# Attention and FP4 feed-forward on one core: row maxima six pair slots ahead of the exps instead of eight

## What is computed

```python
def reference(x, Wqa, Wqb, Wkva, Wkvb, Wout, bout, w_gate, w_up, w_down):
    xn = layernorm(x)
    # attention: 16 heads of 8 features, 4 key/value heads, causal, rotary positions
    q = rope((xn @ Wqa @ Wqb).reshape(b, s, 16, 8))
    kv = (xn @ Wkva @ Wkvb).reshape(b, s, 4, 8, 2)
    k, v = rope(kv[..., 0]), kv[..., 1]          # each repeated for 4 heads
    w = softmax(causal(q k^T * 8 ** -0.5))
    att = (w v) @ Wout + bout
    # feed-forward: inputs and weights of each linear layer are rounded to FP4 in blocks of 16
    h = silu(fp4_linear(xn, w_gate)) * fp4_linear(xn, w_up)
    return x + att + fp4_linear(h, w_down)
```

## Time and profile before

| | us |
|---|---|
| median of 3 runs | 814.58 |
| lowest and highest run | 814.21, 816.49 |
| span of the profiled execution | 812.0 |
| TensorE busy | 731.3 |
| VectorE busy | 637.4 |
| POOL busy | 613.8 |
| ScalarE busy | 545.0 |

### The profile page before, as it was taken

One profiled execution on the slowest core, in us unless ns is written; L12 is line 12 of the kernel. 1 busy time (PEld: TensorE's weight loads), 2 busy tenths in 40 slices (PEclk: granted clock), 3 DMA queues, 4 the chain that ended last, 5 costly groups with the idle time before them and its releaser, 6 DMA issues.

```text
span 812.0 us, 18601 instructions
## 1 busy us (share of the span) xinstructions
PE 731.3 (90%) x6541; PEld 445.5 (55%) x6541; DVE 637.4 (78%) x1378; ACT 545.0 (67%) x1154; POOL 613.8 (76%) x707
## 2 busy tenths in 40 slices
PE   2366989999999999999999999999999999999782
PEld 1233545666656565656656565656566565656242
DVE  5569888989888888889898888888898888788200
ACT  1212777768777777777787777677777777575850
POOL 5533697878788897978787887979787888748470
PEclk9978899999999999999999999999999999999996
DMA  4423233333343334343333433343333433330211
GB/s 112 121 57 102 56 100 97 94 101 100 98 116 93 92 113 101 118 105 90 96 108 99 117 95 84 114 104 113 90 94 102 113 90 100 93 93 29 57 48 41
DMA packets 84438, 76.06 MB, mean 94 GB/s; under 512 B 27282, under 2 KB 66162, under 8 KB 84346
## 3 DMA queue, kind: packets, MB, share of 16 engines
q1 hardware_dynamic: 84346, 74.87, 33.9%
HBM read 40.73 MB, written 27.53 MB: 84 GB/s over the span
## 4 chain that ended last, share of the span: by engine, by line
PE 65%; DVE 8%; ACT 7%; DMA 6%; POOL 5%; issue 4%; SPq 4%; POOLq 0%; ACTq 0%; DVEq 0%
PE pv_ps L1109 16%; PE exp_ps L1088 12%; PE max_ps L1073 9%; PE misc_ps L1125 7%; PE max_ps L1074 5%; PE misc_ps L1166 5%; DVE neg_max L713 4%; PE misc_ps L1133 3%; ACT P L909 3%; DMA o_sum<-o_scr 2%; PE misc_ps L1164 2%; PE misc_ps L1152 2%; SPq L418 2%; PE misc_ps L1142 2%; DMA o_scr<-oT 1%
## 5 line engine op out<-in xcount | busy, mean ns | idle before, releaser
L713 DVE TENSOR_REDUCE neg_max<-max_ps 128x1 f32<-128x512 f32 (+3 forms) x768 | 430.6, 591 | 82.8 <-PE max_ps L1074 80.4
L909 ACT ACTIVATE P<-exp_ps 128x512 f32<-128x512 f32 x512 | 295.0, 599 | 166.4 <-PE exp_ps L1088 166.1
L1088 PE MATMUL exp_ps<-Q,K 128*128 128x512 bf16 (+3 forms) x1024 | 243.6, 301 | 9.0 <-ACT P L909 6.7
L1073 PE MATMUL max_ps<-K,Q 128*128 128x384 bf16 (+2 forms) x768 | 199.4, 278 | 24.6 <-DVE neg_max L713 13.5
L1074 PE MATMUL max_ps<-Kd,Q 128*128 128x128 bf16 x1024 | 190.9, 221 | 1.8 <-DVE neg_max L713 1.6
L529 POOL TENSOR_SCALAR_AFFINE_SELECT P<-P 128x512 f32<-128x512 f32 x256 | 162.8, 673 | 27.1 <-ACT P L912 27.1
L1109 PE MATMUL pv_ps<-P,V 128*32 128x512 f32 (+3 forms) x2048 | 164.2, 438 | 1.0 <-POOL P L529 0.8
L1073 PEld LDWEIGHTS max_ps<-K,Q 128*128 128x128 bf16 x768 | 75.1, 100 | 103.0 <-DVE neg_max L713 53.1
L1074 PEld LDWEIGHTS max_ps<-Kd,Q 128*128 128x128 bf16 x1024 | 97.9, 99 | 45.7 <-issue 23.0
L561 POOL TENSOR_TENSOR h<-gate_sb,up_half 128x352 f32<-128x352 f32 x64 | 59.8, 935 | 64.4 <-DVE gate_sb L726 64.4
L1088 PEld LDWEIGHTS exp_ps<-Q,K 128*128 128x128 bf16 x1024 | 81.8, 98 | 42.1 <-ACT P L909 20.5
(11 more groups left out here) (108 smaller groups left out, 989.7 us busy)
## 6 DMA issues: line engine op xcount, KB each, us to landing
Q<-q_scr SPq DMA_DIRECT2D x64, 224.0 KB
o_scr<-oT SPq DMA_DIRECT2D x32, 256.0 KB, 3.5
q_scr<-q_split SPq DMA_DIRECT2D x16, 384.0 KB, 2.6
Kd<-K SPq DMA_DIRECT2D x64, 96.0 KB
x_in<-x SPq DMA_DIRECT2D x16, 256.0 KB, 4.6
q_scr<-q_split SPq DMA_DIRECT2D x16, 256.0 KB, 2.9
x_res<-x SPq DMA_DIRECT2D x16, 256.0 KB, 5.7
o_raw<-o_scr SPq DMA_DIRECT2D x32, 128.0 KB
```

The source lines that it names most:

```text
L713: nc.vector.tensor_reduce(neg_max[:, pr // 4, i, heads[0]:heads[0] + len(heads), pr % 4], max_ps[r % 3][:, 0:len(heads) * n].rearrange("p ...
L909: nc.scalar.activation(P[g % 2][:, hh + r % 2, col:col + 512], ps[:, :], ACT.Exp, scale=SCALE).then_inc(exp_done, 1)
L1073: nc.tensor.matmul(ps[:, col:col + d], Qt, Kt[:, half, g, 0:d], start=True, stop=True)
L1088: last = nc.tensor.matmul(exp_ps[n % 2][:, col:col + width], K[par][:, half, pr // 2, kb * 128:(kb + 1) * 128], Q[par][:, pr, kb * 128:S], ...
```

## The change

The maxima move two slots back. In slot s TensorE and VectorE work on pair s - 2 of batch T+1 for s of 2 or more, and in slots 0 and 1 on pairs 6 and 7 of batch T (max_place). What hangs on the maxima moves with them:

- split_high on ScalarE: the half of pairs 4 to 7 from slot 0 (after exp tile 0) to slot 2 (after exp tile 1), the other from slot 4 (after tile 2) to slot 6 (after tile 1).
- split_rest on POOL: each goes between the first and second two causal selects of a group (group 0 and group 2).
- mrow1 goes from point 0 to point 2 of slot 2, mrow0 from point 1 to point 2 of slot 6.
- SP: place_max comes after gather_sums instead of ahead of it, and copy_k comes behind place_max, for the half whose maxima are done, instead of behind load_q.

The waits of reduce_tile, max_tile and copy_k use the new offsets.

```diff
--- before.py
+++ after.py
@@ -56,17 +56,23 @@
 MISC = [
     [[("gate0", 0, 1), ("up0", 1, 1)], [("xnT", 1, 2)], []],
     [[("q", 1, 2)], [("gate1", 0, 1), ("up1", 1, 1)], []],
-    [[("mrow1", 0, 0), ("qrot", 1, 2)], [("kk", 0, 2)], []],
+    [[("qrot", 1, 2)], [("kk", 0, 2)], [("mrow1", 0, 0)]],
     [[("gate2", 0, 1), ("up2", 1, 1)], [("v", 1, 2)], []],
     [[("gate3", 0, 1), ("up3", 1, 1)], [], []],
     [[("xqT", 1, 2)], [("out0", 0, -1)], []],
-    [[("out1", 0, -1)], [("mrow0", 1, 1)], []],
+    [[("out1", 0, -1)], [], [("mrow0", 1, 1)]],
     [[("hqT0", 1, 0)], [("hqT1", 0, 0)], [("hqT2", 1, 0)]],
 ]
 
 H_POWERS = [(2, 2), (2, 3), (2, 4), (3, 2)]
 PV_BLOCKS = ((0, 3), (1, 2))
 FIRST_T, LAST_T = -3, B
+LAG = 2
+
+
+def max_place(slot):
+
+    return int(slot >= LAG), (slot - LAG) % NPAIR
 
 
 class Step:
@@ -394,11 +400,11 @@
                                   ap=[[E * S, NSLOT + 1], [NPAIR * S, D], [1, NPAIR // 2 * S]])
                     sp.dma_start(Q[i][r:r + (NSLOT + 1) * D, 4 * hf:4 * hf + 4, :], src).then_inc(qk_loaded[hf], 16)
 
-            def copy_k(T, hf):
-
-
-                T.wait(sp, k_loaded[hf], 16 * LOAD_K, 2, 16 * LOAD_K)
-                T.wait(sp, max_filled, NPAIR * NMAX, 1, (hf + 1) * NPAIR // 2 * NMAX)
+            def copy_k(T, off, hf):
+
+                i = T.par(off)
+                T.wait(sp, k_loaded[hf], 16 * LOAD_K, off, 16 * LOAD_K)
+                T.wait(sp, max_filled, NPAIR * NMAX, off - 1, (hf + 1) * NPAIR // 2 * NMAX)
                 for half in range(2):
                     r, gs = HALF * half, slice(2 * hf, 2 * hf + 2)
                     sp.dma_start(Kd[r:r + MROW, half, gs, :], K[i][r:r + MROW, half, gs, :]).then_inc(qk_loaded[hf], 16)
@@ -457,9 +463,11 @@
                     T.wait(sp, x_bias_done, 1, 0, 0)
                     sp.dma_start(x_res[:, :, :], x[T.batch(0)].rearrange("(c p) e -> p c e", p=128)).then_inc(x_res_loaded, 16)
                 scatter_sums(T, -1, 1)
+                gather_sums(T, -1, 1)
                 if T.has(0):
                     place_max(T, 0, 1)
-                gather_sums(T, -1, 1)
+                if T.has(1):
+                    copy_k(T, 1, 1)
                 scatter_inverses(T, -1, 1)
                 if T.has(2):
                     i = T.par(2)
@@ -479,13 +487,14 @@
                         sp.dma_start(dst, k_split[32 * j:32 * j + 32, :, :]).then_inc(k_written, 16)
                     load_k(T, 0)
                     load_q(T, 0)
-                    copy_k(T, 0)
                 if T.has(-1):
                     store(T, 0)
                 scatter_sums(T, 0, 0)
+                gather_sums(T, 0, 0)
                 if T.has(1):
                     place_max(T, 1, 0)
-                gather_sums(T, 0, 0)
+                if T.has(2):
+                    copy_k(T, 2, 0)
                 if T.has(-1):
                     store(T, 1)
                 if T.has(4):
@@ -495,7 +504,6 @@
                 if T.has(2):
                     load_k(T, 1)
                     load_q(T, 1)
-                    copy_k(T, 1)
 
             iterate(sp, iteration)
             sp.wait_ge(stored, 32 * B)
@@ -520,11 +528,11 @@
             for m in (ident, ident16):
                 nc.gpsimd.affine_select(out=m[:, :], in_=m[:, :], compare_op=ALU.not_equal, fill=1.0,
                                         base=0, pattern=[[-1, 128]], channel_multiplier=1).then_inc(pool_const, 1)
-            def causal(T, off, g):
+            def causal(T, off, g, parts=(0, 1)):
 
                 T.wait(pool, exp_done, NPAIR * NEXP, off, 2 * NEXP * (g + 1))
                 p = P[g % 2]
-                for kb in PV_BLOCKS[0] + PV_BLOCKS[1]:
+                for kb in [kb for part in parts for kb in PV_BLOCKS[part]]:
                     diag = p[:, :, P_COL[kb]:P_COL[kb] + 128]
                     nc.gpsimd.affine_select(out=diag, in_=diag, compare_op=ALU.is_ge, fill=0.0, base=0,
                                             pattern=[[0, GH], [1, 128]], channel_multiplier=-1).then_inc(causal_done, 1)
@@ -580,7 +588,6 @@
 
                 if T.has(-1):
                     causal(T, -1, 3)
-                split_rest(T, 0, 1)
                 hidden(T, 0)
                 if T.has(2):
                     for part in (1, 2, 3):
@@ -595,7 +602,10 @@
 
 
                 if T.has(0):
-                    causal(T, 0, 0)
+                    causal(T, 0, 0, (0,))
+                split_rest(T, 0, 1)
+                if T.has(0):
+                    causal(T, 0, 0, (1,))
                 if T.has(1):
 
                     T.prev().misc_wait(pool, misc_read, "v")
@@ -627,7 +637,6 @@
                     T.wait(pool, k_casts, 2, 2, 2)
                     nc.gpsimd.tensor_tensor(k_split[:, 2, :], k_rest[:, :], k_split[:, 1, :], ALU.subtract).then_inc(k_pool, 1)
                 statistics(T)
-                split_rest(T, 1, 0)
                 hidden(T, 3)
                 if T.has(0):
                     quantize(T, 0, 1, *hs)
@@ -635,7 +644,10 @@
 
 
                 if T.has(0):
-                    causal(T, 0, 2)
+                    causal(T, 0, 2, (0,))
+                split_rest(T, 1, 0)
+                if T.has(0):
+                    causal(T, 0, 2, (1,))
                     quantize(T, 0, 3, *hs)
                 if T.has(0):
                     T.wait(pool, x_res_loaded, 16, 0, 16)
@@ -700,16 +712,17 @@
                 for c, (_, cn) in enumerate(FC):
                     nc.vector.tensor_copy(wdT[0:cn, c, :], exp_ps[0][0:cn, c * E:(c + 1) * E]).then_inc(w_ready, 1)
 
-            def reduce_tile(T, pr, r):
-
-                if not T.has(1):
+            def reduce_tile(T, slot, r):
+
+                off, pr = max_place(slot)
+                if not T.has(off):
                     return
                 heads, i = MAX_TILES[r]
                 n = (i + 1) * 128
-                T.wait(dve, max_filled, NPAIR * NMAX, 1, pr * NMAX + r + 1)
+                T.wait(dve, max_filled, NPAIR * NMAX, off, pr * NMAX + r + 1)
                 if pr % 4 == 0 and r == 0:
 
-                    T.wait(dve, m_split_done, 2, 0, pr // 4 + 1)
+                    T.wait(dve, m_split_done, 2, off - 1, pr // 4 + 1)
                 nc.vector.tensor_reduce(neg_max[:, pr // 4, i, heads[0]:heads[0] + len(heads), pr % 4],
                                         max_ps[r % 3][:, 0:len(heads) * n].rearrange("p (h k) -> p h k", k=n),
                                         AX.X, ALU.max, negate=True).then_inc(max_read, 1)
@@ -981,9 +994,9 @@
                 if (slot, r) == (3, 2) and T.t0 == FIRST_T + 1:
                     act.wait_ge(w_step, 5)
                     nc.scalar.activation(w_mag[:, :], w_raw[:, :], ACT.Copy, scale=2.0 ** 22).then_inc(w_step, 1)
-                if (slot, r) == (0, 0):
+                if (slot, r) == (2, 1):
                     split_high(T, 0, 1)
-                if (slot, r) == (4, 2):
+                if (slot, r) == (6, 1):
                     split_high(T, 1, 0)
                 if slot == 5 and r < NT:
                     normalize_x(T, r)
@@ -1056,17 +1069,18 @@
                 pe.wait_ge(weights_in, 16 * N_WEIGHTS)
                 pe.wait_ge(const_dma, 16 * N_CONST_DMA)
 
-            def max_tile(T, pr, r):
-
-                if not T.has(1):
+            def max_tile(T, slot, r):
+
+                off, pr = max_place(slot)
+                if not T.has(off):
                     return
                 heads, i = MAX_TILES[r]
 
-                T.wait(pe, max_read, NPAIR * NMAX, 1, pr * NMAX + r - 2)
+                T.wait(pe, max_read, NPAIR * NMAX, off, pr * NMAX + r - 2)
                 if pr % 4 == 0 and r == 0:
-                    T.wait(pe, qk_loaded[pr // 4], 16 * (LOAD_Q + COPY_K), 1, 16 * (LOAD_Q + COPY_K))
-                Kt, ps, g, n = K[T.par(1)], max_ps[r % 3], pr // 2, (i + 1) * 128
-                Qt = Q[T.par(1)][:, pr, i * 128:n]
+                    T.wait(pe, qk_loaded[pr // 4], 16 * (LOAD_Q + COPY_K), off, 16 * (LOAD_Q + COPY_K))
+                Kt, ps, g, n = K[T.par(off)], max_ps[r % 3], pr // 2, (i + 1) * 128
+                Qt = Q[T.par(off)][:, pr, i * 128:n]
                 for a, half in enumerate(heads):
                     col, d = a * n, i * 128
                     if i > 0:
```

## The result

| | before | after |
|---|---|---|
| median of 4 runs, us | 814.39 | 861.20 |
| lowest and highest run | 812.84, 816.49 | 857.05, 865.38 |
| span of the profiled execution | 812.0 | 855.0 |

The ratio is 1.057, interval 1.054 to 1.061: 46.8 us slower. The forecast was 824.7 with a range up to 832. So the sign was right, and some 36 us are missing from the sum.

What follows compares the result with a forecast made beforehand. The prediction took TensorE's in-order queue as the bound, each pause adding time. Its terms, -7.3 + 18.2 - 1.9 + 0 + 1.1 = +10.1 us, took 814.6 to 824.7 us, range 816.5 to 832.

Steps and rivals of the forecast that it cites:

- part 3: High split leaves slot 0: 0.12 us less, 16 times, -1.9 us; POOL's moved half costed at nothing, bound 3 us.
- Part 1: Start, before the first exp: side jobs no longer queue behind the wait for Kd; 7.3 us won, bounds 5.5 and 10.
- Part 2: Slot 2: mrow1 behind kk on the same bank waits for k_sin; 14 x 1.3 = 18.2 us slower.
- (a): The wait at mrow1 costs nothing, given back by shorter pauses in slots 0 and 4: 806.5 us, chance 0.09.
- (b): The wait at mrow1 is half, 0.6 us, because VectorE runs ahead: 814.9 us, chance 0.10.
- Part 4: SP's queue, gathering ahead of placing: placing lands with 0.6 us to spare; cost 0, bounds 0 and 5.
- rival (c): The placing lands late at slot 0 in each iteration: 7.5 us more, 832 us, chance 0.11.
- Part 5: The end, T = 15: maxima in slots 0 and 1, placing 0.7 us late; +1.1 us, bounds 0 and 2.5.
- Rival (d): The start wins nothing because q, k and loads of batch 1 set the first exp: 832 us, chance 0.05.

Runs made afterwards that it cites:

- e1: The changed kernel with a filler operation of the split's size put back in its old place on POOL: 822.98 us, 1.0114 of before.
- e2: The kernel before with only the first half's split_rest moved on POOL, from ahead of the last gate product to behind the add: 839.48 us, 1.033 of before.
- e4: The changed kernel with the filler operation on POOL and mrow1 on the other misc bank: 805.38 us, 0.9882 of before.
- e3: The changed kernel with mrow1 on the other misc bank: 841.44 us, 1.0338 of before.
- e5: The changed kernel with mrow1 on the other bank and a wait on POOL for onT ahead of its add: 806.65 us, 0.9898 of before.
- e6: The changed kernel with POOL's add of h and h_mag cut into four column quarters: 822.70 us, 1.0114 of before.

## Why the prediction was right in sign and wrong in size

**The step that failed** is in part 3: "POOL's second half moves in between two causal selects ... I cost it at nothing; without that cover I allow the 0.22 us". I priced the split where it went and not where it left. Where it left, its 0.25 us held POOL's add back until onT had begun; without it, TensorE pays 2.04 us an iteration and, in 7 of 12 iterations, about 1.5 more for the clock. The bound that the prediction allowed for this step was 3 us; taking it back in e1 is worth 38. The size of a moved operation was taken as the bound of its effect, and the effect was eight times that in the pause alone. e2 shows the cost by that move alone, and e1 its removal by putting back an operation of the same size.

Could the trace of before have told? Not its chain of waits, in which a steady iteration has no onT; but the 2049 ns in onT's line above was in that trace. Its slow case, POOL's timeline and VectorE's, before:

```profile
692.50 2.86 POOL L539 TENSOR_TENSOR h<-h,h_mag 128x1408 f32<-128x1408 f32 x1
...
693.86 2.05 DVE L755 TENSOR_TENSOR onT<-o_raw,o_spread 128x512 f32<-128x512 f32 x1
```

There POOL had come first, and onT again ended 0.55 us behind it. With the 0.14 us between the two starts in the usual iteration, this would have been a rival with a price: up to 2.6 us in up to 15 iterations, 39 us.

**Part 1, the start: right.** The first maxima of slot 2 in T = -1 start at 47.67 (forecast 48.0, at the lower clock; the other value was 46.3):

```profile
36.30 2.68 PE L1139 MATMUL misc_ps<-wguT,xqT 128*128 128x352 f32 x4 [1.21 <-ACT xqT L965]
...
47.67 0.35 PE L1087 MATMUL max_ps<-K,Q 128*128 128x384 bf16 x1
...
75.10 0.43 PE exp_ps L1102
```

(The last is of the chain, the others of TensorE's timeline.) The four gate and up matmuls take 2.68 us, as in the earlier trace rows, so the side jobs alone did run at the lower clock. The trace of after has no record of the clock ahead of 47.7 us, and its windows print 1.00 there; e4, where the same four take 2.69 us, has 0.50 (a window as above):

```profile
36.00:46.00 10.00, 6.25 (x12) 3.07 (x12) 3.34 (x8) 3.35 (x8) 4.79 (x5) 0.50 0.60 134
```

The Trainium skill (TensorE: Matmul & The Clock Gate, What's actually happening) has activity release the slow state; the side jobs of this stretch did not bring the 46.3 of the full clock. The first exp starts at 75.10 instead of 81.3, 6.2 us won of the 7.3, and within the bounds. The granted clock between 66 and 75 us is 0.62, so the last maxima before it ran partly at the lower level; before, the 9 us ahead of the first exp had 0.56, so this alone does not explain the missing 1.1 us, and their cause stays open. In e4 the first exp starts at 74.20.

**Part 2, mrow1 behind kk: right in place, size and count**, 18.3 us in 14 waits, with 14 x 1.3 = 18.2 forecast; removed by the other bank in e3. e1 less e4, each against its own runs of before, is 9.2 + 9.3 = 18.5 us. So rivals (a) and (b), that the wait would be given back whole or by half, are out.

**Part 3's other half, slot 0: right in size, from a pause that was misread.** In the chains of waits, from the first maxima of slot 0 to xnT, it was 3.06 us before (394.85 to 397.91, its end in the earlier trace rows) and is 2.94 after (458.30 to 461.24): the 0.12 of the forecast. But the 2.4 us that the prediction takes from the earlier trace rows for a pause of TensorE are a stretch in which the chain runs over ScalarE while TensorE works. Its timeline before:

```profile
395.66 1.35 PE L1125 MATMUL misc_ps<-wguT,xqT 128*128 128x352 f32 x4
...
397.39 0.38 PE L1088 MATMUL exp_ps<-Q,K 128*128 128x384 bf16 x2
397.91 0.66 PE L1129 MATMUL misc_ps<-ident,xn 128*128 128x128 f32 x4
```

TensorE stands idle 0.14 us ahead of 397.91, and 0.02 at the same place after. So 0.12 is nearly all that was there to win, and rival (a) had no 2.4 us that could shrink.

**Part 4, SP's queue: right.** SP's timeline of after shows gathering ahead of placing, as in the sum:

```profile
449.34 0.35 SPq L433 DMA_DIRECT2D o_scr<-oT  x1
451.64 0.58 SPq L443 DMA_DIRECT2D o_sum<-o_scr  x1
453.00 2.50 SPq L424 DMA_DIRECT2D Q<-m_row  x4
```

From the scatter to the end of the placing's issue is 6.2 us here (449.34 to 455.50). Part 4 had 3.5 + 1.2 and four issues of 0.64, 7.3. The scatter lands after a median of 2.0 us instead of the 3.5 of the earlier trace rows. TensorE's exps wait for the placing once, 0.8 us. In e1, with the period of the forecast, the scatter lands after 2.0 to 4.3 us, median 2.8, and the exps wait 1.1 us in 3. So rival (c) is out; it needed 4.1 us of landing in each iteration. The estimate of 2.6 by the Trainium skill (DMA: Bandwidth & Descriptors, Anatomy of one DMA) was nearer to both medians than the row that the sum used.

**Part 5, the end: its 0.7 us is seen in e1**, where the end is not hidden behind the longer pauses. TensorE's timeline in slot 4 of T = 15, with the wait in brackets:

```profile
776.60 0.59 PE L1107 MATMUL exp_ps<-Q,K 128*128 128x512 bf16 x2 [0.67 <-DMA Q<-m_row]
```

For the whole part there is only a remainder: e4's span is 8.2 us shorter than before's, of which the first exp gives 7.1 and 14 x 0.23 gives 3.2, so some 2.1 come back at the end, near the upper bound of 2.5. Which slots take the rest of it was not tried, and neither was where the steady iteration's 0.23 comes from beyond the 0.12 of slot 0.

**Rival (d)**, a start that wins nothing, is out with part 1.

## What to carry to other kernels

An operation that leaves a queue lets those behind it start earlier, up to their next wait, and the place it leaves has to be read as carefully as the one it goes to: look for pairs on VectorE and POOL that start within a few tenths of a microsecond of each other, and for a group whose longest duration is three times its median. A duration that doubles without a wait is a reason to lay the timelines of the other engines beside it. Where such an order matters, hold it by a semaphore, as e5 does, or cut the longer instruction, as e6 does, and give a step that is moved a bank whose reader is already done.

## What the runs showed of the hardware

- VectorE's onT and POOL's add, each with two inputs in SBUF, exclude each other for one instruction's length, with no wait in the profile: onT 0.73 us when it starts 0.14 ahead, 3.33 when it starts 0.06 behind, 1.33 when POOL's instruction is a quarter as long. In three late cases (after, e6 and the slow one of before) it ends 0.54 to 0.55 us behind POOL's instruction.
- A wait of TensorE of 2.04 us in slot 5 was followed by a lower granted clock, 0.72 to 0.75 over the next 6 us, in 7 of 12 iterations, at some 1.5 us each; in e2 it was 3 of the 9 with the long onT (0.72 to 0.74). Why the others kept 1.00 stays open.
